# Three units each of images 0 to 2 sampled by matrix products under the next image's LSTM, in a four-layer image network

## The reference

```
x = x + attention(_gn(x))      # 8x8 blocks, keys and values from a 14x14 window, 4 heads
x = x + lstm(_gn(x))           # 96 rows of an image as a batch, 96 steps, hidden size 128
x = x + deformable(_gn(x))     # 3x3 deformable convolution, bilinear sampling, zero padding
x = x + catalan(_gn(x))        # M . block . M^T on 8x8 blocks
```

```
x_off = g_lt * gather(qx_lt, qy_lt) + g_rb * gather(qx_rb, qy_rb) + g_lb * gather(...) + g_rt * gather(...)
x_off = x_off * m
out   = conv2d(x_off, conv_w, stride=3)
```

## Time and profile before

| | us |
|---|---|
| median of three runs | 3741.62 |
| the profiled execution, own time | 3740.99 |
| its span (first to last instruction) | 3739.2 |

### The profile page before, as it was taken

One profiled execution on the slowest core, in us unless ns is written; L12 is line 12 of the kernel. 1 busy time (PEld: TensorE's weight loads), 2 busy tenths in 40 slices (PEclk: granted clock), 3 DMA queues, 4 the chain that ended last, 5 costly groups with the idle time before them and its releaser, 6 DMA issues.

```text
span 3739.2 us, 56212 instructions
## 1 busy us (share of the span) xinstructions
PE 2640.3 (71%) x20611; PEld 2008.4 (54%) x20611; DVE 2332.4 (62%) x5156; ACT 1175.7 (31%) x2909; POOL 2474.0 (66%) x2553
## 2 busy tenths in 40 slices
PE   6979977886777677757776377667776274677764
PEld 4667754665667355546664255456664243344433
DVE  5754457985555778755555598656554664576654
ACT  4644434443322244323322144333221211111100
POOL 3200037777777777777777777777777777777775
PEclk9989986876776768767767678767667587898986
DMA  6612027653222376532223376432224222222221
GB/s 207 203 43 71 1 66 218 181 141 91 61 53 53 95 219 182 141 78 74 54 53 96 98 204 180 113 84 68 53 53 109 64 66 66 53 53 53 53 53 49
DMA packets 207306, 360.06 MB, mean 96 GB/s; under 512 B 69760, under 2 KB 116640, under 8 KB 207024
## 3 DMA queue, kind: packets, MB, share of 16 engines
q0 software_dynamic: 80352, 164.72, 17.4%
q1 hardware_dynamic: 125288, 191.27, 17.3%
q10 hardware_dynamic: 1392, 0.48, 0.1%
HBM read 261.08 MB, written 94.30 MB: 95 GB/s over the span
## 4 chain that ended last, share of the span: by engine, by line
POOL 58%; issue 19%; DVE 4%; PE 2%; DMA 1%; ACT 1%; POOLq 0%; SPq 0%; DVEq 0%; ACTq 0%
POOL got L716 58%; DMA got<-sample_table,index 1%; DVE got L1099 1%; DVE mx L1210 0%; PE gates L1889 0%; PE gates L1880 0%; DVE samp L1122 0%; PE bank L1522 0%; DVE bank L1109 0%; DVE bank L1101 0%; PE gates L1752 0%; DVE x L1477 0%; PE bank L1621 0%; DVE bank L1111 0%; DMA qst<-q_parts 0%
## 5 line engine op out<-in xcount | busy, mean ns | idle before, releaser
L716 POOL DMA_INDIRECT got<-sample_table,index x2511 | 2419.2, 963 | 1118.1 <-issue 761.0
L1099 DVE TENSOR_TENSOR got<-got,bank 128x864 f32<-128x864 f32 x279 | 292.6, 1049 | 466.2 <-DMA got<-sample_table,index 460.9
L1752 PE MATMUL gates<-hist,whh 128*128 128x96 f32 x2280 | 444.4, 358 | 191.0 <-DVE hist L1391 189.7
L1752 PEld LDWEIGHTS gates<-hist,whh 128*128 128x128 f32 x2280 | 400.7, 264 | 240.2 <-DVE hist L1391 239.3
L1554 PE MATMUL gates<-cells,row_hat 128*128 128x416 f32 x972 | 404.6, 578 | 170.5 <-DVE spanned L1080 169.2
L799 ACT ACTIVATE pt<-gates 98x512 f32<-98x512 f32 x528 | 288.1, 593 | 355.4 <-PE gates L1652 338.5
L1554 PEld LDWEIGHTS gates<-cells,row_hat 128*128 128x128 f32 x972 | 210.5, 222 | 347.3 <-issue 299.9
L1522 PE MATMUL bank<-turned,wout 128*128 128x96 f32 x1728 | 266.6, 321 | 148.7 <-DVE x L1133 77.9
L1210 DVE TENSOR_REDUCE mx<-gates 128x2 f32<-128x392 f32 x576 | 295.6, 553 | 94.6 <-PE gates L1638 93.3
L1522 PEld LDWEIGHTS bank<-turned,wout 128*128 128x128 f32 x1728 | 258.9, 237 | 166.7 <-DVE turned L1127 83.2
L1638 PE MATMUL gates<-kst,qst 96*128 96x196 bf16 x1152 | 187.6, 282 | 122.7 <-DVE mx L1210 105.8
(11 more groups left out here) (180 smaller groups left out, 4397.1 us busy)
## 6 DMA issues: line engine op xcount, KB each, us to landing
kst<-k_parts SPq DMA_DIRECT2D x96, 441.0 KB
got<-sample_table,index POOLq DMA_INDIRECT x2511
qst<-q_parts SPq DMA_DIRECT2D x96, 288.0 KB
k_parts<-kp SPq DMA_DIRECT2D x24, 882.0 KB
k_parts<-kp SPq DMA_DIRECT2D x24, 588.0 KB
q_parts<-qp SPq DMA_DIRECT2D x24, 576.0 KB
sample_table<-tab SPq DMA_DIRECT2D x12, 784.0 KB
q_parts<-qp SPq DMA_DIRECT2D x24, 384.0 KB
```

Of the source, the lines that this page charges most:

```text
L716: pool.indirect_dma_start(out=got[:, g % RING, n, :], out_offset=None, in_=tables[p], in_offset=bass.IndirectOffsetOnAxis(ap=at, axis=0)). ...
L1099: dve.tensor_tensor(corners, corners, w[:, :, 0:3].unsqueeze(3).to_broadcast([P, NTAP, 3, C]), ALU.mult).then_inc(weighted, 1)
L1752: mm = pe.matmul(gate[n][:, h:h + W], whh[:, HID * g:HID * (g + 1)], hist[:, (t - 1) % HIST, :], start=False, stop=True, skip_group_check= ...
```

## The change

- `DENSE_GROUPS` gets one group more in each of images 0, 1 and 2: group 20, units 60 to 62. They are not gathered. `PREPARED` and `ATTENDED` move slightly, and units are counted as before, the new ones among them.
- Their 27 steps of an image (3 units x 9 taps) run inside the next image's LSTM: TensorE issues 162 products from step 14 of the LSTM on, three in an even step, one in an odd one (`pieces_upto`); VectorE does 27 x (two multiplications and one sum), one to three steps later (`SUM_AT`), ahead of the step's point; ScalarE makes the nine row hats, six instructions each (`HAT_AT`).
- The gates' PSUM banks are rearranged (`both_gate`: the gates i and f share bank 2), and banks 4 and 6 take the products of the LSTM (`step_dense_ps`).
- `near` is also stored as plain planes (`planes`), and `cells` is loaded from them with 12 DMAs of 100-byte pieces: for images 0 to 2 after the second chunk of LSTM inputs, for image 3 after `prepare(3)`.
- Row positions are no longer spread by TensorE: TensorE transposes them once (`located_ps`), ScalarE copies, SyncE stores (`locations`), and ScalarE's queue loads them back with a broadcast (`load_spread`, 4 DMAs a unit). This holds for image 3 too. L966 and L1536 go.
- The order in `cells`, PSUM and `spanned` is channel before column, so that the sum over columns (L1083) reads neighbours. `dsamp` holds 6 units, `row_hat` 3 thirds of a unit.
- In `prepare`, 8 turns (`EARLY`, was 4) come ahead of the first offset convolution.

```diff
-EARLY = 4
+EARLY = 8
...
-ATTENDED = (0, 28, 95, 167)
+ATTENDED = (0, 28, 96, 167)
 STEPPED = (0, 59, 127, 199)
-PREPARED = (0, 66, 138, 210)
+PREPARED = (0, 68, 138, 210)
...
-DENSE_GROUPS = (8, 15, 22)
-DENSE = {UNITS * LAST + GUNITS * k + i: GUNITS * d + i for d, k in enumerate(DENSE_GROUPS) for i in range(GUNITS)}
+DENSE_GROUPS = tuple((p, 20) for p in range(LAST)) + ((LAST, 8), (LAST, 15), (LAST, 22))
...
+HATS = 3
+SPREADS = 2
+SAMPLES = 2 * GUNITS
...
+FIRST_PIECE = 14
+FIRST_HAT = 8
...
+def pieces_upto(t):
+
+    n = t - FIRST_PIECE + 1
+    return min(max(4 * (n // 2) + 3 * (n % 2), 0), PIECES * GSTEPS)
+
+
+def step_points():
+
+    sums = []
+    for s in range(GSTEPS):
+        half = [next(t for t in range(W) if pieces_upto(t) >= PIECES * s + KTILES * (h + 1)) for h in range(2)]
+        sums += [half[0] + 1, half[1] + 1, half[1] + 2]
+    hats = [FIRST_HAT + NTAP * n + i for n in range(3 * GUNITS) for i in range(2 * KTILES)]
+    return sums, hats
...
+                    if k == 1 and p > 0:
+                        load_cells(p - 1)
...
+                sp.dma_start(planes[p].rearrange("c (j r) s -> j c (r s)", j=J), near[:, 1:1 + R, :].rearrange("p r s -> p (r s)")).then_inc(
+                    plane_stored, 16)
+                for i, d in enumerate(groups_of(p)):
+                    sp.wait_ge(rows_copied, d + 1)
+                    sp.dma_start(locations[d], located[:, i, :]).then_inc(rows_stored, 16)
+
+            def load_cells(p):
+                sp.wait_ge(plane_stored, 16 * (p + 1))
                 for t in range(KTILES):
                     for a in range(CELLS):
-                        for first, last, j, r in band_rows(t):
-                            sp.dma_start(cells[32 * a + first:32 * a + last, t],
-                                         pixels[j, r:r + last - first, CELL * a + 1:CELL * a + 1 + FINE, 0:C]).then_inc(cells_in, 16)
+                        sp.dma_start(cells[32 * a:32 * (a + 1), t],
+                                     planes[p][:, 32 * t:32 * (t + 1), CELL * a + 1:CELL * a + 1 + FINE].rearrange("c y f -> y c f")).then_inc(
+                                         cells_in, 16)
...
+                hats_done = 0
+                if p > 0:
+                    for v in range(GUNITS * (p - 1), GUNITS * (p - 1) + SPREADS):
+                        load_spread(v)
...
+                    while p > 0 and hats_done < len(HAT_AT) and HAT_AT[hats_done] <= t:
+                        n, i = hats_done // (2 * KTILES), hats_done % (2 * KTILES)
+                        row_hat_part(3 * GUNITS * (p - 1) + n, i, GUNITS * p)
+                        hats_done += 1
...
+                for i, d in enumerate(groups_of(p)):
+                    act.wait_ge(rows_turned, d + 1)
+                    wait(act, rows_stored, 16 * d if i == 0 else 0)
+                    act.activation(located[:, i, :], located_ps[i], ACT.Copy).then_inc(rows_copied, 1)
...
+            def load_spread(v):
+                d, u = v // GUNITS, v % GUNITS
+                act.wait_ge(rows_stored, 16 * (groups_of(DENSE_GROUPS[d][0])[-1] + 1))
+                wait(act, hat_begun, 3 * KTILES * (v - SPREADS + 1))
+                rows = locations[d].rearrange("(u n a) s -> u a n s", u=GUNITS, a=CELLS)
+                for a in range(CELLS):
+                    act.dma_start(spread[32 * a:32 * (a + 1), v % SPREADS], rows[u, a].unsqueeze(0).to_broadcast([32, NTAP, P])).then_inc(
+                        spread_in[v % SPREADS], 16)
...
+            def row_hat_part(n, i, units):
                 v, h = n // 3, n % 3
...
+                t = i % KTILES
+                to = row_hat[:, n % HATS, t].rearrange("p n s -> p (n s)")
+                if i == 0:
+                    act.wait_ge(spread_in[v % SPREADS], 16 * CELLS * (v // SPREADS + 1))
+                    wait(act, dense_filled, 2 * TAPS3 * (n - HATS + 1))
+                if i < KTILES:
+                    of = spread[:, v % SPREADS, TAPS3 * h:TAPS3 * (h + 1), :].rearrange("p n s -> p (n s)")
+                    act.activation(to, of, ACT.Abs, bias=trows[:, t:t + 1]).then_inc(hat_begun, 1)
+                    return
+                act.wait_ge(hat_begun, KTILES * n + t + 1)
+                act.activation(to, to, ACT.Relu, bias=ccols[:, 0:1], scale=-1.0).then_inc(hat_ready, 1)
+                if (h, i) == (2, 2 * KTILES - 1) and v + SPREADS < units:
+                    load_spread(v + SPREADS)
...
-            def dense_sum(s):
+            def dense_sum(s, h):
                 v, n = s // NTAP, s % NTAP
-                dve.wait_ge(dense_filled, s + 1)
-                wait(dve, dense_summed, s)
-                for h, (a, b) in enumerate(FINES):
-                    dve.tensor_tensor(spanned[:, a:b, :], dense_ps[s % 2][h][:, 0:C * (b - a)].rearrange("p (f c) -> p f c", c=C),
-                                      col_hat[:, v, n, a:b].unsqueeze(2).to_broadcast([P, b - a, C]), ALU.mult).then_inc(dense_read, 1)
+                d, u = v // GUNITS, v % GUNITS
+                if h < 2:
+                    dve.wait_ge(dense_filled, 2 * s + h + 1)
+                    wait(dve, dense_summed, s)
+                    dve.tensor_tensor(spanned[:, C // 2 * h:C // 2 * (h + 1), :], sums_of(s, h).rearrange("p (c f) -> p c f", f=FINE),
+                                      hats_of(d)[:, u, n, :].unsqueeze(1).to_broadcast([P, C // 2, FINE]), ALU.mult).then_inc(dense_read, 1)
+                    return
                 dve.wait_ge(dense_read, 2 * s + 2)
-                dve.tensor_reduce(dsamp[:, v, n, :], spanned[:, :, :].rearrange("p f c -> p c f"), AX.X, ALU.add).then_inc(dense_summed, 1)
+                if n == 0 and v >= SAMPLES:
+                    dve.wait_ge(samp_turned, DENSE_UNIT[v - SAMPLES] + 1)
+                dve.tensor_reduce(dsamp[:, v % SAMPLES, n, :], spanned[:, :, :], AX.X, ALU.add).then_inc(dense_summed, 1)
...
+                    while p > 0 and dense_done < 3 * GSTEPS * p and SUM_AT[dense_done - 3 * GSTEPS * (p - 1)] <= t:
+                        dense_sum(dense_done // 3, dense_done % 3)
+                        dense_done += 1
                     point()
...
+            def dense_piece(s, h, t):
+                v, n = s // NTAP, s % NTAP
+                late = s >= LSTEPS
+                if (h, t) == (0, 0):
+                    if s % GSTEPS == 0:
+                        pe.wait_ge(cells_in, 16 * KTILES * CELLS * min(v // GUNITS + 1, B))
+                    pe.wait_ge(hat_ready, KTILES * (3 * v + n // TAPS3 + 1))
+                if t == 0:
+                    wait(pe, dense_read, 2 * (s - (2 if late and s >= LSTEPS + 2 else 1)) + h + 1)
+                mm = pe.matmul(sums_of(s, h), row_hat[:, 3 * v % HATS + n // TAPS3, t, n % TAPS3, :],
+                               cells[:, t, C // 2 * h:C // 2 * (h + 1), :].rearrange("p c f -> p (c f)"), start=(t == 0), stop=(t == KTILES - 1))
+                if t == KTILES - 1:
+                    mm.then_inc(dense_filled, 1)
...
+                    while p > 0 and pieces_done < pieces_upto(t):
+                        s, at = GSTEPS * (p - 1) + pieces_done // PIECES, pieces_done % PIECES
+                        dense_piece(s, at // KTILES, at % KTILES)
+                        pieces_done += 1
...
+                for i, d in enumerate(groups_of(p)):
+                    pe.wait_ge(dense_ready, d + 1)
+                    pe.transpose(located_ps[i], cell_rows[:, i].rearrange("p u n a -> p (u n a)"),
+                                 ident[:, :]).then_inc(rows_turned, 1)
```

More of the change, by code:

```diff
@@ L217, in dense_points @@
     held = steps[resting + REST[0] - 1]
-    ahead = [min(n + 2, held if i < resting + REST[0] + NT + 1 else DSTEPS) if n else 0 for i, n in enumerate(steps)]
+    ahead = [min(n + 2, held if i < resting + REST[0] + NT + 1 else DSTEPS) if n > LSTEPS else LSTEPS for i, n in enumerate(steps)]
     return steps, ahead, held
@@ L476, in network @@
         dense_ready = sem("dense_ready")
[L477 to L479 removed]
+        plane_stored = sem("plane_stored")
+        rows_turned = sem("rows_turned")
+        rows_copied = sem("rows_copied")
+        rows_stored = sem("rows_stored")
+        spread_in = [sem(f"spread_in{i}") for i in range(SPREADS)]
         hat_begun = sem("hat_begun")
@@ L986, in _, with row_hats @@
+            def row_hats(n):
+                for i in range(2 * KTILES):
+                    row_hat_part(n, i, DUNITS)
             for p in range(B):
@@ L989, in _ @@
                 prepare(p)
-            act.wait_ge(tab_stored, 16 * len(TSTORES) * B)
-            act.wait_ge(chain, MATH * len(CHUNK_OF))
-            act.wait_ge(dense_consts_in, 32)
-            row_hats(0)
+            begin = GUNITS * LAST
+            for later in range(begin, begin + SPREADS):
+                load_spread(later)
+            for n in range(3 * begin, 3 * begin + HATS):
+                row_hats(n)
             transform(0)
             transform(1)
-            row_hats(1)
```

(28 more changed lines are left out.)

156 lines of the change are left out of this document (67 added, 89 removed).

## The result

The changed kernel takes 3654.04 us (median of 4 runs, 3651.73 to 3659.93) against 3740.68 for the kernel before on the same chip. The ratio is 0.977, with a 95% interval of 0.9752 to 0.9787. The forecast was 3661, 7 us too high, in a range of 3638 to 3712.

What follows compares the result with a forecast made beforehand. GpSimd's gathers were taken to bound the kernel, other stages mattering only through their lead. The sum was 3741 - 102 (gathers) + 6 (`prepare(0)`) + 16 (stall at image 2) = 3661 us, range 3638 to 3712.

Steps and rivals of the forecast that it cites:

- The 102 us for 81 gathers: GpSimd's gathers: 9 of 279 units removed, so 81 gathers fewer, taken as 102 us less.
- `prepare(0)`, +6: Image 0's preparation: one more group of positions on VectorE takes 6.0 us, so GpSimd's 7.5 us stall grows by 6.
- The LSTMs, +20 each: LSTMs of images 1 to 3: +5 dense steps, +4 DMA issues, +1.5 last sum, +10 lower-clock spells; ends 0 and 50.
- The sum, 1.1 us: VectorE's sum over columns: reading neighbours, 1.1 us for 800 elements, against 1.51 at a pitch of 32.
- `prepare(1)`, +7: Image 1's preparation: 6.0 us for the positions on VectorE and 1 us for their transpose, copy and store.
- `prepare(2)`, +7: Image 2's preparation: 6.0 us for the positions on VectorE and 1 us for their transpose, copy and store.
- Stall of 16 at image 2: Head of image 2's attention: GpSimd's lead reaches 7.4 units against a limit of 6, so it stops 16 us.
- No stop after that: From image 2's to image 3's attention: VectorE's stages need 750 us, GpSimd 767, so the lead falls; same for image 3.
- The signs: If right: 2430 gathers at 1.25 to 1.28 us, GpSimd waiting 20 to 35, LSTMs 370 to 385, clock over 0.9.
- The lower clock: Rival: TensorE stays at the lower clock in the LSTMs, steps 2.6 us longer; 3888 us with half of them; chance 0.09.
- The loss of 50 us an LSTM: Rival: the LSTMs slow down by 50 us each, still a gain, 3704 us; chance 0.15 for 3688 to 3730.
- slower gathers: Rival: new VectorE work in the LSTMs holds GpSimd, up to 135 us on top, 3793, half of that 3726; chance 0.04.

Runs made afterwards that it cites:

- Experiment 1: Changed kernel with the new groups of images 0 to 2 taken out and the rest of the change kept: 3740.73 us, ratio 0.9999 to the kernel before.
- experiment 2: Changed kernel with only image 0's new group kept, those of images 1 and 2 taken out: 3711.36 us, ratio 0.9925 to the kernel before.
- experiment 9: Changed kernel with a fourth group of image 3 sampled by products: 3624.29 us, ratio 0.9692; with `PREPARED` at 66 as well 3633.27 us.
- experiment 8: The changed kernel, unaltered, run and profiled again: 3652.08 us, ratio 0.9768 to the kernel before.
- experiment 7: Changed kernel with only the convolution of group 20 in `prepare(1)` issued one point later, after both halves of the offset chunk: 3645.44 us, ratio 0.9755.
- experiment 3: Kernel before, with spare matmuls also in the LSTMs of images 1 to 3 and no products there: 3739.63 us, ratio 1.0007.
- experiment 4: Changed kernel with the sum over columns made twice in the 81 steps under the LSTMs: 3699.61 us, ratio 0.9902 to the kernel before.
- experiment 5: Changed kernel with `RING = 5` in place of 6, room for five units of gathers: 3687.38 us, ratio 0.9864 to the kernel before.
- experiment 6: Changed kernel with `PREPARED = (0, 66, 138, 210)`, moving group 20's convolution and sampling two units fewer in `prepare(1)`: 3660.21 us, ratio 0.978.

## Why the prediction was right

- **The 102 us for 81 gathers.** Right as a mechanism. Experiment 1 takes it away and the gain is 0; experiments 2 and 9 price a group of 27 gathers at 28 us each, all stalls and positions included, against 34 for the gathers alone.
- **`prepare(0)`, +6.** The stage grew by 5.8, and the stall at the head of attention 1 by 4.4 in the profiled execution and 5.6 in that of experiment 8.
- **The LSTMs, +20 each.** Mis-sized. They came out at -4, -3 and +4. The start was right: the first hidden state comes 15.3 us into the stage before and 18.4 after, and +4 was given for the loads of `spread`. A step with products was laid out as 3.63 us against 3.57; the 81 of them took 3.45, 3.44 and 3.55 us each (from the starts of L1468). The 10 us for spells at the lower clock were not paid there: the windows with products show 1.00 or 0.99. In the old stages VectorE waited 0, 13 and 17 us for gathers, which covered part of the new work; less these waits, the LSTMs changed by -4, +10 and +19. So in LSTM 3 nearly all of the +20 was there, and it took the place of a wait.
- **The sum, 1.1 us.** Measured 0.983, the multiplication 0.567 for 0.55. By the rule on 16-byte lines that the prediction cited (the Trainium skill, "SBUF — State Buffer", section "Door 1: The DMA port swizzle"), the sum over neighbours should be cheaper. The trace agrees: 1.510 us fell to 0.983 for the same 800 elements.
- **`prepare(1)`, +7.** Mis-sized the other way: +15.4. The prediction counted the new instructions and missed what `PREPARED` does to the order: it moves a convolution between two halves of the offsets (10 us, experiment 7: 92.5 us fell to 82.3).
- **`prepare(2)`, +7.** Here the stage less its waits for gathers grew from 80 to 96 us, +16, and VectorE's wait for ScalarE's copy of the offset convolution (L1522, before L1439) went from 2.7 to 21.7 us. With the LSTM's +10 the cycle from attention 2 to attention 3 comes to 747 us less waits; the prediction had 750. The sum was right and its two parts were not. Why this wait grew was not tried.
- **Stall of 16 at image 2.** The mechanism, lead against limit, was right, and its inputs were not: the stall was 7.2. VectorE arrives later by -4 and +15 instead of +20 and +7, 11 us in place of 27, which is 1.0 unit instead of 2.4. With that the prediction's count gives 4.0 + 1.0 + 1 = 6.0, exactly the limit and no stall; the trace has a lead of 6.0 and the 7.2 us. Near the limit the count does not give the size of a stall.
- **No stop after that.** Right: the leads are 5.3 in attention 3 and 5.8 at the first transform, with 0 us of stall (1.4 at the transform in experiment 8). It was closer than the prediction's surplus of 17 us a cycle made it look.
- **The total.** 3741 - 102 + 11 of stalls + 10 of slower gathers = 3660, the profiled execution. The median is 6 us lower. The stalls were forecast 11 us too high (22 against 11) and the gathers up to 10 us too low: two errors that cancelled. That the number lies within 7 us is luck to that extent; the 102 us and the ring's stalls are not.
- **The signs.** Gathers (2430 at 1.278 us, from 521), clock (0.92 over the stage), sum and VectorE's waits (350 us) came as said. Two signs of being right did not: LSTM stages of 370 to 385 us (352 to 362), and GpSimd's wait of 20 to 35 us (18.3, and 20.4 in experiment 8).
- **Rivals.** The lower clock did not come: the cause that the prediction had against it (the products fill the same gaps as the spare matmuls of the first LSTM) fits the windows, and experiment 3 shows that by itself the clock is worth nothing. What the products would cost at the lower clock was not run. The loss of 50 us an LSTM was priced too low, at 3704: experiment 4 has LSTMs only 16, 19 and 31 us longer than before and takes 3700 already. It confirms that lateness is paid as stalls, but at three heads and not at one or two as priced, since the changed kernel's leads are at 5.3 to 6.0 already. The price of slower gathers, 3793, is 3661 + 135 = 3796 by its own terms. Slower gathers did not come: in the three LSTMs, beside the new work, a gather took 0.957, 0.962 and 0.963 us in the mean (0.960, 0.958 and 0.959 in experiment 8), and 0.959, 0.957 and 0.957 before. The longest one in the quiet stretch is 0.957 us, and 0.953 before. The Trainium skill ("SBUF — State Buffer", section "SBUF: two separate sides") describes the lock for a VectorE instruction in a two-port mode, and says there that `tensor_tensor`, the multiplication, has no such mode and that `tensor_reduce`, the sum, never contends with GpSimd on trn2. The trace agrees.

```profile
L768 POOL DMA_INDIRECT got<-sample_table,index x433: 943/947/957, 3059.1 to 3599.4; - x145
```

What stays open: the gathers' 10 us. Experiment 4, with as many products, has a mean of 0.964 us, and a median of 0.944 in the quiet stretch, as the kernel before. So the products are not the cause of the 0.947 above; part of it goes with the execution. The slowest gathers are those beside the attentions, 0.98 to 1.00 us in the mean in both kernels. In attention 2 they went from 0.980 to 0.994 us (0.997 in experiment 8), which is 3 of the 10 us; why was not tried.

## What to carry to other kernels

Where one engine works through a fixed list behind a ring, its time is its list plus its stalls. Here a faster consumer was worth nothing (experiments 1 and 3), a list shorter by 27 gathers, 34 us, was worth 28 after the stalls that came with it (2 and 9), and the consumer's lateness cost time only where the lead touched the ring (4 and 5). Count the lead at the head of each stage, before and after.
A number that sets how much is done in a stage also moves what is queued between other work: change the place by itself before you judge it (6 against 7).

## What was not expected of the hardware

- The 27 steps of products cost an LSTM some 46 us, and the clock that came with them (0.99 to 1.00 in their windows, 0.69 to 0.71 before) gave 28 to 50 back; both by the estimate of experiment 3.
- The same spare matmuls that gave 1.00 in the first LSTM brought the clock only to 0.90 or 0.91 in the later ones, where VectorE waits 43 to 48 us for gathers. Why was not tried.
- A sum over 800 neighbours takes 0.983 us, with a pitch of 32 elements 1.510.
